# A cap of two gathers under way in the edge loops of a two-layer graph kernel

## The chip, the cores and the metric

The kernel runs on one core of one Trainium2 chip. The metric is the device time of one execution, in microseconds (us). Three runs of the kernel before gave a median of 5060.37 us (5058.44 to 5061.42).

## The reference

There are 6250 nodes with 128 features and 206,250 edges (100,000 random pairs in both directions, and one loop per node), sorted by destination. Two layers follow one another:

```
h = relu(layernorm(x))
# layer 0, per edge e = (row = src[e], col = dst[e]), 8 heads of 16
att = exp(clip(sum_d((h[row] @ Wq) * (h[col] @ Wk)), -10, 10))
res[row] += att / (sum of att over the row) * (h[col] @ Wv)
x = x + layernorm(res + h) * gamma + beta
h = relu(layernorm(x))
# layer 1
alpha = beta1 * dot(h[row], h[col]) / (|h[row]| |h[col]|)
out[row] = sum(softmax over the row's edges of alpha * h[col])
x = x + out
```

So each layer reads, for each edge, a whole row of a table by the edge's `col`.

## The kernel before

`sort_and_project` sorts the edges by `row` into tiles of 128 edges and makes the table `kv` (256 float32 per node) in DRAM. `layer0_edges` walks over the edges, `between_layers` makes the next table `h1` (130 float32 per node), `layer1_edges` walks over the edges again, and `finish` writes the output.

Both edge loops go over 417 groups (`GROUPS`) of `GT` = 4 tiles. For a tile, POOL issues one indirect DMA, a gather, that fetches 128 rows of the table into the 128 partitions of one slot of the ring `G` (`gather_groups`, line 892). The ring holds 8 groups in the first loop (`RING0`, tile name kv_rows) and 12 in the second (`RING1`, h_rows). The other engines work some groups behind, each by its own counted semaphores. `walk` writes one turn of the loop out in Python and repeats it with a hardware loop: the turn is 16 groups in the first loop (`HAND0`) and 24 in the second (`HAND1`), for POOL, DVE, ACT and SP.

Once a turn the last tile of the last group isn't gathered by POOL: SP fetches its 128 rows one by one into the buffer `hand` (`hand_rows`, lines 1023 and 1467; 8 of them per group in the first loop, up to 6 in the second), and ACT copies them into the ring (lines 1088 and 1522). `by_hand(u, t, period)` says whether a group is such a one. It then has three gathers, j = 0, 1, 2.

The order on POOL within a group is: wait until ACT has written the group's indices (`s_idx`), wait until the ring's slot is free (`s_read`: DVE's line 1195 in the first loop, PE's line 1586 in the second), add 1 to `s_go`, and then four gathers in a row with no wait between them. An addition to `s_go` is an instruction of its own on the queue, and the waits before it are on it. Each gather adds 16 to the semaphore of its ring slot (`s_gat[k]`, 8 semaphores in the first loop, 12 in the second), one for each of 16 DMA engines, when its data has landed. `gathers_of` counts how many gathers of the slot lie at or before a group, and DVE waits for 16 times that before the first use of the group (lines 1177 and 1657): in the first loop the product at line 1182, in the second the cosines at line 1633.

Of the kernel before, what the change touches and what calls it, by code (L numbers as in the profile page):

```python
# [45 lines left out]
GT = 4  # L46
# [9 lines left out]
HALF = UPG // 2  # L56
# [5 lines left out]
RING0 = 8  # L62
RING1 = 12
# [11 lines left out]
HAND0 = 16  # L75
BYHAND = P // HAND0
COPY0_AT = 12
HAND1 = 2 * RING1
# [791 lines left out]
    return u == period - 1 and not (isinstance(t, int) and t == 0)  # L870


def gathers_of(t, u, ring, period):

    each, now = GT * (period // ring), GT * (u // ring + 1)
    if u % ring < ring - 1 or isinstance(t, int) and t == 0:
        return each * t + now
    return (each - 1) * t + now + (u < period - 1)


def gather_groups(pool, ring, table, G, idx, s_idx, s_read, s_gat, s_go, period=None):

    def step(i, u, t):
        if not inside(i):
            return
        k = u % ring
        hand = period is not None and by_hand(u, t, period)
        pool.wait_ge(s_idx, i + 1)
        need(pool, s_read, i - ring + 1)
        pool.sem_inc(s_go, 1)  # L890
        for j in range(GT - hand):
            pool.indirect_dma_start(out=G[:, k, j, :], out_offset=None, in_=table,  # L892
                                    in_offset=bass.IndirectOffsetOnAxis(ap=idx[:, k, j:j + 1], axis=0)
                                    ).then_inc(s_gat[k], 16)
    walk(pool, step, period or ring, first=0, drain=0)


def own_quad(dram, q, n):
# [18 lines left out]
def layer0_edges(nc, mem, dram):  # L917

    with ExitStack() as ctx:
# [37 lines left out]
        s_across = sem("s_across")  # L957
        s_decoded = sem("s_decoded")
        s_idx = sem("s_idx0")
        s_gat = [sem(f"s_gat0_{k}") for k in range(RING0)]  # L960
        s_part = sem("s_part0")
        s_turned = sem("s_turned0")
        s_bytile = sem("s_bytile0")
# [174 lines left out]
        def _(dve):  # L1138
# [28 lines left out]
            def step(i, u, t):  # L1167
                if inside(i + 4):
                    k = u % NEAR
                    dve.wait_ge(s_spread, i + 5)  # L1170
                    need(dve, s_q, i + 5 - NEAR)
                    if inside(i):
                        dve.wait_ge(s_own, i + 1)
                    nc.vector.tensor_scalar(hotT[:, k, :], B_ps[u % 2], part_no[:, 0:1], None,
                                            ALU.is_equal).then_inc(s_hotT, 1)
                if inside(i):
                    dve.wait_ge(s_gat[u % RING0], 16 * gathers_of(t, u, RING0, HAND0))
                    if by_hand(u, t, HAND0):
                        dve.wait_ge(s_copied, t)
                    dve.wait_ge(s_q, i + 1)  # L1180
                    need(dve, s_red, i)
                    nc.vector.tensor_tensor(prod[:, :].rearrange("p (j f) -> p j f", f=D),
                                            Q_ps[u % NEAR].rearrange("p (j f) -> p j f", f=D),
                                            G[:, u % RING0, :, 0:D], ALU.mult).then_inc(s_prod, 1)
                if inside(i):
                    dve.wait_ge(s_prod, i + 1)
                    need(dve, s_clip, i + 1 - NEAR)
                    nc.vector.reduce_sum(att[:, u % NEAR, :],
                                         prod[:, :].rearrange("p (a d) -> p a d", d=HD), AX_X).then_inc(s_red, 1)
                if inside(i - 2):  # L1190
                    k = (u - 2) % NEAR
                    dve.wait_ge(s_ex, i - 1)
                    need(dve, s_sum, i - 1 - NEAR)
                    v = vx[:, k, :, :]
                    nc.vector.tensor_tensor(v[:, :, 0:D].rearrange("p j (h d) -> p j h d", d=HD),
                                            G[:, (u - 2) % RING0, :, D:2 * D].rearrange("p j (h d) -> p j h d", d=HD),
                                            v[:, :, D:AW0].unsqueeze(3).broadcast_to((P, GT, HEADS, HD)),
                                            ALU.mult).then_inc(s_vx, 1)
                if inside(i - 4):
                    for h in range(HALF):  # L1200
                        add_unit(i, u, t, h)
                if inside(i - 2):
                    nc.vector.tensor_tensor(hot[:, k, :].rearrange("p (j n) -> p j n", n=P),
                                            over(loc_f[:, ds(GT * (i - 2), GT)], P), under(iota[:, :], GT),
                                            ALU.is_equal).then_inc(s_hot, 1)
                if inside(i):
                    dve.wait_ge(s_red, i + 1)
                    need(dve, s_ex, i + 1 - NEAR)
                    nc.vector.tensor_scalar(clip[:, u % NEAR, :], att[:, u % NEAR, :], -10.0, 10.0,  # L1209
                                            ALU.max, ALU.min).then_inc(s_clip, 1)  # L1210
                if inside(i - 4):
                    for h in range(HALF, UPG):
                        add_unit(i, u, t, h)
# [159 lines left out]
def layer1_edges(nc, mem, dram):  # L1373
# [3 lines left out]
    with ExitStack() as ctx:  # L1377
# [44 lines left out]
        s_ids = sem("s_ids1")  # L1422
        s_hand = [sem(f"s_hand1_{k}") for k in range(2)]
        s_copied = sem("s_copied1")
        s_gat = [sem(f"s_gat1_{k}") for k in range(RING1)]
        s_own = [sem(f"s_own_{k}") for k in range(RING1 // FOUR)]
        s_hotT = sem("s_hotT1")
        s_hot = sem("s_hot1")
# [171 lines left out]
        def _(dve):  # L1600
# [38 lines left out]
            def step(i, u, t):  # L1639
                if inside(i - 9):  # L1640
                    for h in range(HALF):
                        add_unit(i, u, t, h)
                if inside(i - 6):
                    k = (u - 6) % SOON
                    dve.wait_ge(s_E, i - 5)
                    need(dve, s_wgt, i - 5 - SOON)
                    nc.vector.tensor_tensor(below[:, k, :], logit[:, (u - 6) % RING1, :], E_ps,
                                            ALU.subtract).then_inc(s_below, 1)
                if inside(i - 9):
                    for h in range(HALF, UPG):  # L1650
                        add_unit(i, u, t, h)
                if inside(i - 4):
                    dve.wait_ge(s_L, i - 3)
                    nc.vector.reduce_max(highs[:, ds(UPG * (i - 4), UPG), 1:2].rearrange("p u o -> p (u o)"),  # L1654
                                         L_ps[u % 2].rearrange("p (h e) -> p h e", h=UPG), AX_X).then_inc(s_gmax, 1)
                if inside(i):
                    dve.wait_ge(s_gat[u % RING1], 16 * gathers_of(t, u, RING1, HAND1))
                    if by_hand(u, t, HAND1):
                        dve.wait_ge(s_copied, t)
                    dve.wait_ge(s_q, i + 1)  # L1660
                    need(dve, s_logit, i + 1 - SOON)
                    need(dve, s_prod, i)
                    cosines(u, 0, GT // 2)
                if inside(i - 4):
                    w, v = (u - 4) % RING1, (u - 4) % SOON
                    before = 0.0 if isinstance(i, int) and i == 4 else tops[:, (u - 5) % RING1, UPG - 1, 1:2]
                    dve.wait_ge(s_gmax, i - 3)
                    need(dve, s_newtop, i - 4)
                    units = slice(UPG * (i - 4), UPG * (i - 3)) if isinstance(i, int) else ds(UPG * (i - 4), UPG)
                    nc.vector.tensor_tensor_scan(tops[:, w, :, :].rearrange("p u k -> p (u k)"),  # L1670
                                                 same[:, units, :].rearrange("p u k -> p (u k)"),
                                                 highs[:, units, :].rearrange("p u k -> p (u k)"),
                                                 before, ALU.mult, ALU.max).then_inc(s_newtop, 1)
                if inside(i):
                    cosines(u, GT // 2, GT).then_inc(s_prod, 1)
                if inside(i - 4):
                    dve.wait_ge(s_newtop, i - 3)
                    need(dve, s_corr, i - 3 - SOON)
                    nc.vector.tensor_tensor(fall[:, v, :], tops[:, w, :, 0:1].rearrange("p u o -> p (u o)"),
                                            tops[:, w, :, 1:2].rearrange("p u o -> p (u o)"),  # L1680
                                            ALU.subtract).then_inc(s_fall, 1)
                if inside(i):
                    need(dve, s_hotw, i + 1 - RING1)
                    nc.vector.tensor_tensor(hot[:, u % RING1, :, :], under(loc_b[:, ds(GT * i, GT)], P),
                                            iota_j[:, :, :], ALU.is_equal).then_inc(s_hot, 1)
# [93 lines left out]
```

## Time and profile before

| | |
|---|---|
| median of 3 runs | 5060.37 us |
| profiled execution: span on the page (it gives no other time) | 7130.1 us |
| first loop, first to last gather | 686.9 to 3894.4 us, 1643 gathers |
| second loop, first to last gather | 4052.2 to 7053.7 us, 1652 gathers |
| POOL, share of the span | 47% |
| PE, DVE, ACT | 61%, 58%, 34% |

The profiled execution is one run under the hardware profiler, and its span is 2070 us longer than the median. Its rows give durations and distances of single instructions. A row of the timeline is: start us, duration us, engine, line, operation, output<-input, and in brackets the idle time of the engine before it with what ended it.

### The profile page before, as it was taken

The numbers are of one execution on the slowest core, as the hardware profiler recorded it, in microseconds if no ns is written. First come the engines' busy times: TensorE is split into PE (matmuls) and PEld (weight loads), VectorE is DVE, ScalarE is ACT, GpSimd is POOL, SyncE is SP. The second block draws the span as 40 slices with busy tenths as digits, with TensorE's granted clock in tenths as the row PEclk, the third lists the DMA queues.
The fourth block names the chain that finished last, engine by engine and source line by source line (L and its number), as shares of the span: only waits on it lengthen the run. The fifth ranks groups of instructions, "written<-read, shape, count | busy, mean of one in ns | idle before, by whom it ended". The sixth has DMA issues, their size and how long they took to land. (4 is left out here: it accounts for less than half of the span.)

```text
span 7130.1 us, 118004 instructions
## 1 busy us (share of the span) xinstructions
PE 4342.2 (61%) x22945; PEld 3749.1 (53%) x22946; DVE 4103.2 (58%) x12176; ACT 2444.7 (34%) x8557; POOL 3380.1 (47%) x3426
## 2 busy tenths in 40 slices
PE   6997555555555555555455156677667676666665
PEld 3886344434443444434344156676666676666665
DVE  8998555555555555555556545555555555555555
ACT  4997111111110111111011544454454444444443
POOL 1334555545454554545454245555555555555552
PEclk8998666666666666666666576666676666776666
DMA  1001222222222222222222112121221121112111
GB/s 35 25 23 34 81 80 76 77 75 77 74 79 77 77 77 75 77 75 79 77 76 73 38 43 48 46 48 47 48 47 47 47 49 46 47 47 49 46 45 39
DMA packets 211652, 414.52 MB, mean 58 GB/s; under 512 B 69399, under 2 KB 103640, under 8 KB 211068
## 3 DMA queue, kind: packets, MB, share of 16 engines
q0 software_dynamic: 135184, 326.41, 17.4%
q1 hardware_dynamic: 74048, 79.04, 3.8%
q10 hardware_dynamic: 1836, 4.03, 0.2%
q14 instruction: 553, 4.53, 0.2%
q8 instruction: 31, 0.51, 0.0%
HBM read 363.52 MB, written 42.48 MB: 57 GB/s over the span
## 5 line engine op out<-in xcount | busy, mean ns | idle before, releaser
L892 POOL DMA_INDIRECT kv_rows<-kv_table,idx_ring x1643 | 1624.6, 989 | 1590.9 <-issue 1003.7
L892 POOL DMA_INDIRECT h_rows<-h_table,idx_ring x1652 | 1566.7, 948 | 1592.7 <-issue 1029.9
L1132 PE MATMUL psum<-vx,hot 128*128 128x136 f32 x3336 | 864.0, 411 | 1135.6 <-DVE acc L1165 1041.0
L1132 PEld LDWEIGHTS psum<-vx,hot 128*128 128x128 f32 x3336 | 696.2, 287 | 1280.3 <-DVE acc L1165 1140.8
L1628 DVE SCALAR_TENSOR_TENSOR h_sb<-h_sb,corr,psum 128x129 f32 x1668 | 582.8, 349 | 931.8 <-PE psum L1586 496.4
L1165 DVE TENSOR_TENSOR acc<-acc,psum 128x136 f32 x1668 | 489.4, 293 | 1006.2 <-remote 850.0
L1576 PE MATMUL psum<-ident,hotl 128*128 128x128 f32 x1668 | 393.9, 381 | 952.7 <-DVE highs L1654 880.6
L1080 ACT ACTIVATE vx<-clip 128x32 f32<-128x32 f32 x417 | 95.2, 229 | 2332.1 <-DVE clip L1209 1878.7
L1576 PEld LDWEIGHTS psum<-ident,hotl 128*128 128x128 f32 x1668 | 258.5, 192 | 1030.6 <-issue 895.4
L1121 PE MATMUL psum<-q_sb,hotT 128*128 x3336 | 712.0, 380 | 32.9 <-issue 23.0
L1121 PEld LDWEIGHTS psum<-q_sb,hotT 128*128 128x128 f32 x3336 | 607.5, 273 | 184.7 <-issue 184.7
L1586 PE MATMUL psum<-h_rows,hotw 128*128 128x129 f32 x3336 | 685.2, 373 | 3.3 <-DVE h_sb L1628 2.7
L1567 PE MATMUL psum<-q_sb,acc 128*128 x3336 | 634.8, 350 | 40.4 <-issue 21.5
L1515 ACT ACTIVATE logit<-cosb,cb_sb 128x4 f32<-128x4 f32 x417 | 124.0, 297 | 1559.6 <-DVE prod L1633 1313.2
L1586 PEld LDWEIGHTS psum<-h_rows,hotw 128*128 128x128 f32 x3336 | 650.1, 288 | 4.9 <-issue 3.3
L1594 PEld LDWEIGHTS psum<-tops,acc 128*128 128x128 f32 x3336 | 585.1, 263 | 0.0
L1567 PEld LDWEIGHTS psum<-q_sb,acc 128*128 128x128 f32 x3336 | 555.6, 251 | 42.9 <-issue 42.8
L1594 PE MATMUL psum<-tops,acc 128*128 128x1 f32 x3336 | 548.8, 286 | 0.0
L1507 ACT ACTIVATE hotl<-hot,logit 128x128 f32<-128x128 bf16 x1668 | 536.9, 392 | 0.0
L1507 ACT ACTIVATE hotw<-hot,wgt 128x128 f32<-128x128 bf16 x1668 | 536.2, 392 | 0.2
L1633 DVE SCALAR_TENSOR_TENSOR prod<-psum,h_rows 128x128 f32<-128x128 f32 x1668 | 509.5, 343 | 40.4 <-remote 35.5
L597 ACT ACTIVATE ends<-is_place,pk_now 128x96 f32<-128x96 bf16 x1260 | 460.7, 467 | 59.6 <-DVE is_place L771 58.0
(225 smaller groups left out, 5834.1 us busy)
## 6 DMA issues: line engine op xcount, KB each, us to landing
hand<-kv_table SPq DMA_DIRECT2D x3200, 1.0 KB
hand<-h_table SPq DMA_DIRECT2D x2048, 0.5 KB
own_rows<-own SPq DMA_DIRECT2D x104, 256.0 KB
own<-own_rows SPq DMA_DIRECT2D x104, 256.0 KB
h_rows<-h_table,idx_ring POOLq DMA_INDIRECT x1652
kv_rows<-kv_table,idx_ring POOLq DMA_INDIRECT x1643
kv_table<-kv SPq DMA_DIRECT2D x21, 256.0 KB, 2.1
out<-q_sb SPq DMA_DIRECT2D x2, 1536.0 KB
```

Of the source, the lines that this page charges most:

```text
L597: last = nc.scalar.activation(to_place[:, k, c, :], is_place[:, k, :, c], ACT.Copy, scale=pk_now[:, r, BATCH * b + c:BATCH * b + c + 1])
L892: pool.indirect_dma_start(out=G[:, k, j, :], out_offset=None, in_=table, in_offset=bass.IndirectOffsetOnAxis(ap=idx[:, k, j:j + 1], axis=0 ...
L1121: last = nc.tensor.matmul(Q_ps[k][:, j * P:(j + 1) * P], hotT[:, k, j * P:(j + 1) * P], q_sb[:, ds(blks[j], 1), :].rearrange("p o f -> p ( ...
L1132: last = nc.tensor.matmul(S_ps[j // HALF][:, j % HALF, :], hot[:, k, j * P:(j + 1) * P], vx[:, k, j, :], start=True, stop=True)
L1165: nc.vector.tensor_tensor(sums, sums, S_ps[h // HALF][:, h % HALF, :], ALU.add).then_inc(s_acc, 1)
L1507: last = nc.scalar.activation(out[:, j * P:(j + 1) * P], hot[:, u, :, j], ACT.Copy, scale=scale[:, j:j + 1])
L1567: last = nc.tensor.matmul(Q_ps[k][:, j * P:(j + 1) * P], hotT[:, (u + 1) % RING1, j * P:(j + 1) * P], q_sb[:, ds(blks[j], 1), :].rearrange ...
L1576: last = nc.tensor.transpose(L_ps[u % 2][:, j * P:(j + 1) * P], hotl[:, (u - 2) % TRIO, j * P:(j + 1) * P], ident[:, :])
L1586: last = nc.tensor.matmul(S_ps[j // HALF][:, j % HALF, :], hotw[:, (u - 8) % TRIO, j * P:(j + 1) * P], G[:, (u - 8) % RING1, j, 0:AW1], st ...
L1594: last = nc.tensor.matmul(E_ps[:, j:j + 1], hotT[:, n, j * P:(j + 1) * P], tops[:, n, j, 1:2], start=True, stop=True)
L1628: nc.vector.scalar_tensor_tensor(sums, sums, corr[:, (u - 9) % RING1, h:h + 1], S_ps[h // HALF][:, h % HALF, :], ALU.mult, ALU.add).then_i ...
L1633: last = nc.vector.scalar_tensor_tensor(prod[:, j * P:(j + 1) * P], Q_ps[u % 2][:, j * P:(j + 1) * P], G[:, u % RING1, j, D + 1:TW], G[:, ...
```

## The change

POOL gets a wait ahead of each gather. Gathers are split by the parity of their tile j in the group, and there are two semaphores, `s_gat[0]` for the even tiles and `s_gat[1]` for the odd ones, in place of one for each slot of the ring. Before the gather of tile j POOL waits until all gathers of the same parity issued so far have landed, and adds 1 to `s_go`. Only the first two gathers of a loop have no such wait. DVE's wait for a group becomes two waits, one for each parity. A group that is fetched partly by hand lacks its gather j = 3, an odd one. Nothing is changed in what is computed, in the ring's sizes or in the other engines.

```diff
-def gathers_of(t, u, ring, period):
+def gathers_of(t, u, period, parity):
 
-    each, now = GT * (period // ring), GT * (u // ring + 1)
-    if u % ring < ring - 1 or isinstance(t, int) and t == 0:
+    each, now = HALF * period, HALF * (u + 1)
+    if parity == 0 or isinstance(t, int) and t == 0:
         return each * t + now
     return (each - 1) * t + now + (u < period - 1)
 
+def landed(eng, s_gat, t, u, period):
+
+    for parity in range(2):
+        eng.wait_ge(s_gat[parity], 16 * gathers_of(t, u, period, parity))
...
         pool.sem_inc(s_go, 1)
+        asked = [gathers_of(t, u, period, parity) - HALF + (hand and parity == 1) for parity in range(2)]
         for j in range(GT - hand):
+            if j >= 2 or not (isinstance(i, int) and i == 0):
+                pool.wait_ge(s_gat[j % 2], 16 * (asked[j % 2] + j // 2))
+                pool.sem_inc(s_go, 1)
             pool.indirect_dma_start(out=G[:, k, j, :], out_offset=None, in_=table,
                                     in_offset=bass.IndirectOffsetOnAxis(ap=idx[:, k, j:j + 1], axis=0)
-                                    ).then_inc(s_gat[k], 16)
+                                    ).then_inc(s_gat[j % 2], 16)
...
-                    dve.wait_ge(s_gat[u % RING0], 16 * gathers_of(t, u, RING0, HAND0))
+                    landed(dve, s_gat, t, u, HAND0)
...
-                    dve.wait_ge(s_gat[u % RING1], 16 * gathers_of(t, u, RING1, HAND1))
+                    landed(dve, s_gat, t, u, HAND1)
```

## Rows read from the trace of the kernel before

**Rows 1.** The page's part 1: busy time, share of the span, instructions.
```profile
PE 4342.2 (61%) x22945; PEld 3749.1 (53%) x22946; DVE 4103.2 (58%) x12176; ACT 2444.7 (34%) x8557; POOL 3380.1 (47%) x3426
```

**Rows 2.** Line 892: duration ns min/median/max, first and last start us.
```profile
L892 POOL DMA_INDIRECT h_rows<-h_table,idx_ring x1652: 938/944/1855, 4052.2 to 7053.7; - x184
L892 POOL DMA_INDIRECT kv_rows<-kv_table,idx_ring x1643: 940/946/1725, 686.9 to 3894.4; - x183
```

**Rows 3.** Waits of all engines: waited for, us in total, times, longest us.
```profile
POOL kv_rows L892 <- DVE vx L1195: 580.0, 149, 15.3
...
ACT kv_rows L1088 <- DMA hand<-kv_table: 517.9, 24, 25.4
...
POOL h_rows L892 <- PE psum L1586: 335.4, 110, 7.3
...
DVE prod L1182 <- ACT kv_rows L1088: 264.8, 25, 13.3
```

**Rows 4.** Timeline, first loop: DVE's pace when it catches up, and SP's.
```profile
2004.44 0.75 DVE L1174 TENSOR_SCALAR hotT<-psum,part_no 128x512 f32<-128x512 f32 x1
...
2004.93 25.02 SPq L1023 DMA_DIRECT2D hand<-kv_table  x28
...
2009.00 0.75 DVE L1174 TENSOR_SCALAR hotT<-psum,part_no 128x512 f32<-128x512 f32 x1
```

**Rows 5.** Timeline of POOL, first loop: gathers in a row, then a pause.
```profile
2039.94 0.95 POOL L892 DMA_INDIRECT kv_rows<-kv_table,idx_ring  x1 [0.30 <-issue]
2041.19 0.95 POOL L892 DMA_INDIRECT kv_rows<-kv_table,idx_ring  x1 [0.30 <-issue]
2042.44 0.95 POOL L892 DMA_INDIRECT kv_rows<-kv_table,idx_ring  x1 [0.30 <-issue]
2043.69 0.94 POOL L892 DMA_INDIRECT kv_rows<-kv_table,idx_ring  x1 [0.30 <-issue]
2044.94 0.95 POOL L892 DMA_INDIRECT kv_rows<-kv_table,idx_ring  x1 [0.30 <-issue]
```

**Rows 6.** Quarter microseconds after the gather at 2044.94; DMA share and GB/s stand last.
```profile
2045.94:2046.19 0.25, 0.00 (x0) 0.00 (x0) 0.00 (x0) 0.00 (x0) 0.00 (x0) 0.50 0.07 21
...
2046.44:2046.69 0.25, 0.00 (x0) 0.00 (x0) 0.00 (x0) 0.00 (x0) 0.00 (x0) 0.50 0.43 98
...
2046.94:2047.19 0.25, 0.00 (x0) 0.00 (x0) 0.00 (x0) 0.00 (x0) 0.00 (x0) 0.50 0.49 197
2047.19:2047.44 0.25, 0.00 (x0) 0.00 (x0) 0.00 (x0) 0.00 (x0) 0.00 (x0) 0.50 0.02 0
2047.44:2047.69 0.25, 0.00 (x0) 0.00 (x0) 0.00 (x0) 0.00 (x0) 0.00 (x0) 0.50 0.00 0
```

**Rows 7.** The same in the second loop, after a last gather at 5412.87.
```profile
5414.62:5414.87 0.25, 0.00 (x0) 0.00 (x0) 0.00 (x0) 0.00 (x0) 0.00 (x0) 0.50 0.51 117
5414.87:5415.12 0.25, 0.00 (x0) 0.00 (x0) 0.00 (x0) 0.00 (x0) 0.00 (x0) 0.50 0.02 0
5415.12:5415.37 0.25, 0.00 (x0) 0.00 (x0) 0.06 (x1) 0.00 (x0) 0.00 (x0) 0.50 0.00 0
```

**Rows 8.** Timeline: from a releaser's end to the gather that it releases.
```profile
2052.37 0.68 DVE L1195 TENSOR_TENSOR vx<-kv_rows,vx 128x512 f32<-128x512 f32 x1
...
2053.86 1.26 POOL L892 DMA_INDIRECT kv_rows<-kv_table,idx_ring  x1 [7.98 <-DVE vx L1195]
...
5453.84 1.85 PE L1586 MATMUL psum<-h_rows,hotw 128*128 128x129 f32 x8
...
5456.51 0.94 POOL L892 DMA_INDIRECT h_rows<-h_table,idx_ring  x1 [2.33 <-PE psum L1586]
```

**Rows 9.** Timeline of POOL, second loop: the next two heads of groups after 5456.51.
```profile
5463.18 0.94 POOL L892 DMA_INDIRECT h_rows<-h_table,idx_ring  x1 [1.86 <-PE psum L1586]
...
5469.77 0.94 POOL L892 DMA_INDIRECT h_rows<-h_table,idx_ring  x1 [1.90 <-remote]
```

**Rows 10.** The page's costliest groups: busy, mean ns, idle before with its releaser.
```profile
L892 POOL DMA_INDIRECT kv_rows<-kv_table,idx_ring x1643 | 1624.6, 989 | 1590.9 <-issue 1003.7
```

More of the change, by code:

```diff
@@ L870, in by_hand, with gather_groups @@
     return u == period - 1 and not (isinstance(t, int) and t == 0)
-def gathers_of(t, u, ring, period):
-    each, now = GT * (period // ring), GT * (u // ring + 1)
-    if u % ring < ring - 1 or isinstance(t, int) and t == 0:
+def gathers_of(t, u, period, parity):
+    each, now = HALF * period, HALF * (u + 1)
+    if parity == 0 or isinstance(t, int) and t == 0:
         return each * t + now
     return (each - 1) * t + now + (u < period - 1)
-def gather_groups(pool, ring, table, G, idx, s_idx, s_read, s_gat, s_go, period=None):
+def landed(eng, s_gat, t, u, period):
+    for parity in range(2):
+        eng.wait_ge(s_gat[parity], 16 * gathers_of(t, u, period, parity))
+def gather_groups(pool, ring, table, G, idx, s_idx, s_read, s_gat, s_go, period):
     def step(i, u, t):
@@ L886, in step @@
         k = u % ring
-        hand = period is not None and by_hand(u, t, period)
+        hand = by_hand(u, t, period)
         pool.wait_ge(s_idx, i + 1)
@@ L890, in step @@
         pool.sem_inc(s_go, 1)
+        asked = [gathers_of(t, u, period, parity) - HALF + (hand and parity == 1) for parity in range(2)]
         for j in range(GT - hand):
+            if j >= 2 or not (isinstance(i, int) and i == 0):
+                pool.wait_ge(s_gat[j % 2], 16 * (asked[j % 2] + j // 2))
+                pool.sem_inc(s_go, 1)
             pool.indirect_dma_start(out=G[:, k, j, :], out_offset=None, in_=table,
                                     in_offset=bass.IndirectOffsetOnAxis(ap=idx[:, k, j:j + 1], axis=0)
-                                    ).then_inc(s_gat[k], 16)
-    walk(pool, step, period or ring, first=0, drain=0)
+                                    ).then_inc(s_gat[j % 2], 16)
+    walk(pool, step, period, first=0, drain=0)
 def own_quad(dram, q, n):
@@ L959, in layer0_edges @@
         s_idx = sem("s_idx0")
-        s_gat = [sem(f"s_gat0_{k}") for k in range(RING0)]
+        s_gat = [sem(f"s_gat0_{n}") for n in range(2)]
         s_part = sem("s_part0")
@@ L1424, in layer1_edges @@
         s_copied = sem("s_copied1")
-        s_gat = [sem(f"s_gat1_{k}") for k in range(RING1)]
+        s_gat = [sem(f"s_gat1_{n}") for n in range(2)]
         s_own = [sem(f"s_own_{k}") for k in range(RING1 // FOUR)]
```

## The prediction

> **What bounds the kernel now.** I read the page's busy shares first, then the gathers' line, the waits, and the timeline of POOL. No engine is full: POOL is busy 47% of the span, PE 61% [rows 1]. This page alone doesn't name the bound, since the profiled execution is 2070 us longer than the median of the runs. So the question is which part of the profile also holds without the profiler. In the timeline gathers that follow one another start 1.25 us apart: 0.95 us of work and 0.30 us between them [rows 5]. If the loops went at that pace throughout, they would take (1643 + 1652) x 1.25 = 4119 us [rows 2]. Outside them lie 686.9 us before the first gather, 157.8 us between the loops and 76.4 us from the last gather to the end of the span of 7130.1 us, 921 us together [rows 2]. The sum is 5040 us, 20 us under the measured median of 5060. I take it that in an ordinary run POOL's issue of gathers, 1.25 us each, is the bound in both loops from end to end.
>
> In the profiled execution it isn't: the first loop takes 3207.5 us for 417 groups, 7.7 us each, against 63 gathers of 1.25 us per 16 groups, 4.9 us each. POOL fills the ring and then waits for DVE and PE (580.0 and 335.4 us), ACT waits for the rows fetched by hand (517.9 us) and DVE for ACT (264.8 us) [rows 3]. SP's 28 small transfers take 25.02 us there, 0.89 us each and 7.1 us for the 8 of a group; DVE needs 4.56 us per group when it catches up [rows 4]. So rows of single instructions carry the sum, and the long idle times of this trace don't.
>
> **The change part by part.** The sum is the profiled execution's own rows at the pace without stalls, 5040 us, and the difference is put on the median, 5060. Its own time is the span, 7130.1 us; the page gives nothing around it.
>
> *The wait for the landing.* This is the whole effect. Gather n is released when gather n-2 has landed. What must pass between the starts of n-2 and n is the time from a gather's start to its landing, and the time from a release to the start of the released gather.
>
> Start to landing: after the last gather before a pause the DMA engines can be watched alone. For the gather at 2044.94 they carry its data from 2046.44 on and fall silent in the quarter that begins at 2047.19, 2.25 to 2.50 us after its start; the traffic up to 2046.19 belongs to the gather before [rows 6]. In the second loop, with rows of half the size, they fall silent 2.00 to 2.25 us after the start at 5412.87 [rows 7]. I take 2.40 and 2.20 us. These gathers had no successor behind them, so nothing in this time is a queue that a shallower queue would shorten.
>
> Release to start: the gather at 2053.86 starts 0.81 us after DVE's line 1195 ended (2052.37 + 0.68), the one at 5456.51 starts 0.82 us after PE's line 1586 ended (5453.84 + 1.85) [rows 8]. In the kernel before this time is hidden, since POOL's queue is worked ahead of the gathers; behind a wait that ends last it is exposed each time. That is 3.21 and 3.02 us. How long the semaphore takes to rise after the last traffic, no row shows. Its lower bound is 0; as its upper one I take 0.15 us, since the nearest row, DVE's end to POOL's start, is 0.81 us with the dispatch in it and leaves little room for a longer notice. I add 0.09 and 0.08 us and get 3.30 and 3.10 us for two gathers, 1.65 and 1.55 us for one, against 2.50 and 1.25 us. The wait therefore does end last, by 0.8 and 0.6 us.
>
> The count: even tiles are never taken out by hand, so each loop has a chain of 2 x 417 = 834 even gathers, each released by the one before. The odd chain has fewer and runs beside it. The loops take 834 x 3.30 = 2752 us and 834 x 3.10 = 2585 us, 5338 us together, against 4119. The change costs 1219 us, and the time is 5060 + 1219 = 6279 us.
>
> The Trainium skill (DMA: Bandwidth & Descriptors, section "Anatomy of one DMA — SWDGE (gpsimd) path") gives a DMA from this engine about 2.0 us fixed plus its bytes by 436e3 per us, and says that a wait on a semaphore stands on the issuing sequencer before dispatch. That is 2.30 us for 131,072 bytes and 2.15 us for 66,560, a little under the rows, and as an estimate the sum would come to 834 x (3.11 + 2.97) = 5071 us in the loops, some 6012 us in all. The rule speaks against the change as the rows do.
>
> *The added instructions on POOL.* One addition to `s_go` and one wait per gather, and the arithmetic of the waited value. Behind them on POOL's queue stand all later gathers, and for these DVE waits. At the head of a group POOL's queue already works through two waits and one addition, and gathers in a row keep their 1.25 us across the heads: of five in a row at least one is a head, and all five start 1.25 us apart [rows 5]. So they cost nothing beside a gather in progress. Behind a wait, only the addition that holds it lies on the path, and it is in the 0.81 us. Bounds: 0, and if all of it were exposed 0.1 us per step of the chain, 1668 x 0.1 = 167 us. I take 0.
>
> *DVE's wait becomes two.* 834 more waits. DVE needs 4.56 us per group [rows 4] and would get one every 6.6 and 6.2 us, so this is covered; without that cover it would be under 0.1 us per group, 80 us.
>
> *Fewer semaphores, by-hand groups.* The counting is exact for each parity, so a group is released with its own gathers and no other. After a by-hand group the next even gather waits for the gather just before it; it is in the even chain all the same and adds nothing.
>
> *What is late next.* In the second loop PE and its partners also set a pace: the heads of groups at 5456.51, 5463.18 and 5469.77 us lie 6.67 and 6.59 us apart in this profiled trace [rows 8, 9], more than the 6.2 us that the gathers would give. In ordinary runs this pace must be lower, since the median leaves only about 5 us per group. Slower arrival of work could bring some of it back. I leave it to the range and a rival.
>
> **The rivals.**
>
> 1. *The landing is hidden (about 5060 us).* If outside the profiler a gather landed 0.8 us sooner in the first loop and 0.6 us sooner in the second, the wait would be over before POOL gets to it. For it: the profiler does lengthen SP's transfers and perhaps every DMA. Against it: the gathers' own pace fits the unprofiled median to 20 us, and 1.5 us of the 2.4 pass before the first byte moves [rows 6], on POOL's side of the transfer. 4%.
>
> 2. *Faster (about 4990 us).* POOL's instructions average 989 ns in the first loop against a median of 946 (1624.6 us over 1643 gathers) [rows 2, 10]. If long ones came from several gathers under way at once, a cap would save up to 0.043 x 1643 = 71 us. It decides only where the two-gather chain is under 2.50 us. The landing rows stand against it. 2%.
>
> 3. *PE takes over in the second loop (about 6450 us).* If the slower arrival brings the second loop to the profiled pace of some 6.6 us, it takes 417 x 6.6 = 2752 us in place of 2585, 167 us more: 6446 us. The heads of [rows 9] speak for it. Against it: those groups follow stalls of the profiled execution, and an ordinary run does a group in 5 us. 15%.
>
> 4. *A short chain (about 5850 us).* The gathers land 0.25 us sooner without the profiler: 1668 x 0.25 = 417 us less, 5862 us. 14%.
>
> 5. *The cap isn't one of two.* If the counts let three through, three gathers would share 3.3 us, 1.1 us each, under 1.25, and nothing would change: 5060 us. The values in the diff are those of all earlier gathers of a parity, and the by-hand one is taken off. 1%.
>
> **How the numbers follow.** My forecast, 6279 us, has 64%. Its own ends: silence at 2.25 and 2.00 us after the start gives 834 x (3.06 + 2.82) = 4904 us and 5845 in all; silence at 2.50 and 2.25 us and 0.15 us to notice it gives 834 x (3.46 + 3.22) = 5571 us and 6512. With the short chain and PE's pace in it, the range is 5850 to 6520 us. A change of 0.2% (10 us) is about what a measurement of this kernel can tell from none. Slower: 64 + 15 + 14 = 93%. Same: rivals 1 and 5, 5%. Faster: 2%.
>
> **What would show it right or wrong.** In the new trace POOL's gathers should start about 1.65 us apart in the first loop and 1.55 us in the second, with 0.6 to 0.7 us of idle time before them instead of 0.30 us, ended by a gather's landing or marked as issue; their own 0.95 us should stay. Runs of gathers 1.25 us apart should be gone but for pairs: in an uneven chain one distance may be 1.25 us and the next 2.05. POOL's long waits for DVE and PE should shrink, since 6.6 us per group is close to the 7.7 us that the profiled first loop takes anyway. For the same reason the profiled span should grow far less than the median, to 7130 to 7700 us. If gathers still start 1.25 us apart, the landing is hidden and I am wrong. If they are 1.65 us apart but the median stays near 5060, POOL's issue was never the bound of ordinary runs.

## The result, and the profile after

The changed kernel takes 6800.83 us (median of 3 runs, 6793.10 to 6804.32), against 5060.37 us before. The ratio is 1.343, with a 95% interval of 1.342 to 1.345. The prediction was 6279 us, with a range of 5850 to 6520 us: the sign and the mechanism came as forecast, the size didn't. The change costs 1740 us where 1219 were expected.

The page of the new trace, its parts 1 and 5, with POOL's lines (busy, mean ns, idle before with its releaser), answers to [rows 1, 10]:

```profile
span 6802.6 us, 125599 instructions
...
PE 4908.2 (72%) x22945; PEld 4132.4 (61%) x22946; DVE 4139.0 (61%) x12176; ACT 2447.8 (36%) x8557; POOL 3328.7 (49%) x3426
...
L902 POOL DMA_INDIRECT kv_rows<-kv_table,idx_ring x1643 | 1580.5, 962 | 1482.2 <-DMA kv_rows<-kv_table,idx_ring 905.5
L902 POOL DMA_INDIRECT h_rows<-h_table,idx_ring x1652 | 1559.5, 944 | 1438.2 <-DMA h_rows<-h_table,idx_ring 850.5
```

Most of POOL's idle time is now ended by its own gathers (905.5 of 1482.2 us and 850.5 of 1438.2 us), as predicted. The view of waits also puts 234.9 us, 204 times, on ACT's write of the indices; that write isn't what POOL waits for, since ACT writes the indices of a group eight groups ahead, and from the ninth group on each is done at least 32 us before the group's first gather. The new line of the gathers (duration ns min/median/max, first and last start us), which answers to [rows 2], and what DVE waits for:

```profile
L902 POOL DMA_INDIRECT h_rows<-h_table,idx_ring x1652: 938/942/1857, 3872.0 to 6739.4; - x184
L902 POOL DMA_INDIRECT kv_rows<-kv_table,idx_ring x1643: 940/944/1662, 687.1 to 3741.8; - x183
...
  DVE prod L1192: 986.2, 411
  DVE prod L1643: 967.8, 408
```

The last two rows stand under "who waited for it": DVE now waits for the gathers in almost every group (411 and 408 times in 417). The loops take 3741.8 - 687.1 = 3054.7 us and 6739.4 - 3872.0 = 2867.4 us. Over the 834 even gathers of each that is 3.66 and 3.44 us per step of the chain, against 3.30 and 3.10 us in the prediction.

The timeline of POOL in the first loop answers to [rows 5]:

```profile
2000.32 0.95 POOL L902 DMA_INDIRECT kv_rows<-kv_table,idx_ring  x1 [0.30 <-issue]
2002.58 1.02 POOL L902 DMA_INDIRECT kv_rows<-kv_table,idx_ring  x1 [1.31 <-DMA kv_rows<-kv_table,idx_ring]
2003.91 0.94 POOL L902 DMA_INDIRECT kv_rows<-kv_table,idx_ring  x1 [0.30 <-issue]
2006.23 0.94 POOL L902 DMA_INDIRECT kv_rows<-kv_table,idx_ring  x1 [1.37 <-DMA kv_rows<-kv_table,idx_ring]
2007.47 0.95 POOL L902 DMA_INDIRECT kv_rows<-kv_table,idx_ring  x1 [0.30 <-issue]
```

The reader is to see two interleaved chains: each gather starts 3.56 to 3.65 us after the one two before it (2002.58 to 2006.23, 2003.91 to 2007.47). The gathers' own work stays at 0.95 us. Here the chains run unevenly, so that one distance is short, 1.24 to 1.33 us, and the next 2.3 us.

### The profile page after: what moved, and what is told of

It is laid out like the page before. It is cut to its first block and busy times, and to the rows that moved or that the text cites. A ratio compares the mean times of both kernels' runs of the same rounds, so it can differ in the third digit from the quotient of the medians.

```text
span 6802.6 us, 125599 instructions
## 1 busy us (share of the span) xinstructions
PE 4908.2 (72%) x22945; PEld 4132.4 (61%) x22946; DVE 4139.0 (61%) x12176; ACT 2447.8 (36%) x8557; POOL 3328.7 (49%) x3426
## 5 line engine op out<-in xcount | busy, mean ns | idle before, releaser
L902 POOL DMA_INDIRECT kv_rows<-kv_table,idx_ring x1643 | 1580.5, 962 | 1482.2 <-DMA kv_rows<-kv_table,idx_ring 905.5
L902 POOL DMA_INDIRECT h_rows<-h_table,idx_ring x1652 | 1559.5, 944 | 1438.2 <-DMA h_rows<-h_table,idx_ring 850.5
L1142 PE MATMUL psum<-vx,hot 128*128 128x136 f32 x3336 | 1051.4, 470 | 906.5 <-DVE acc L1175 883.5
L1142 PEld LDWEIGHTS psum<-vx,hot 128*128 128x128 f32 x3336 | 787.3, 321 | 1160.0 <-DVE acc L1175 1110.9
L1192 DVE TENSOR_TENSOR prod<-psum,kv_rows 128x512 f32<-128x512 f32 x417 | 288.5, 692 | 991.7 <-DMA kv_rows<-kv_table,idx_ring 986.2
L1131 PE MATMUL psum<-q_sb,hotT 128*128 x3336 | 861.0, 439 | 39.4 <-issue 38.9
L1131 PEld LDWEIGHTS psum<-q_sb,hotT 128*128 128x128 f32 x3336 | 739.2, 326 | 223.9 <-issue 223.9
L1577 PE MATMUL psum<-q_sb,acc 128*128 x3336 | 681.7, 368 | 204.7 <-DVE prod L1643 195.3
L1596 PE MATMUL psum<-h_rows,hotw 128*128 128x129 f32 x3336 | 724.6, 389 | 2.7 <-DVE h_sb L1638 2.7
L1577 PEld LDWEIGHTS psum<-q_sb,acc 128*128 128x128 f32 x3336 | 590.1, 265 | 223.0 <-issue 221.6
L1596 PEld LDWEIGHTS psum<-h_rows,hotw 128*128 128x128 f32 x3336 | 693.5, 305 | 4.4 <-issue 3.3
```

The costliest lines, as they stand in the source:

```text
L1131: last = nc.tensor.matmul(Q_ps[k][:, j * P:(j + 1) * P], hotT[:, k, j * P:(j + 1) * P], q_sb[:, ds(blks[j], 1), :].rearrange("p o f -> p ( ...
L1142: last = nc.tensor.matmul(S_ps[j // HALF][:, j % HALF, :], hot[:, k, j * P:(j + 1) * P], vx[:, k, j, :], start=True, stop=True)
L1577: last = nc.tensor.matmul(Q_ps[k][:, j * P:(j + 1) * P], hotT[:, (u + 1) % RING1, j * P:(j + 1) * P], q_sb[:, ds(blks[j], 1), :].rearrange ...
L1596: last = nc.tensor.matmul(S_ps[j // HALF][:, j % HALF, :], hotw[:, (u - 8) % TRIO, j * P:(j + 1) * P], G[:, (u - 8) % RING1, j, 0:AW1], st ...
```

## The experiments

**The kernel before, again.** The first trace had a span 2070 us over the median, and the whole baseline was an inference from it. No edit.

> The kernel before, unchanged, for a second trace. Theory (POOL's issue bounds ordinary runs, and the stalls of the first trace belong to that one execution): span near 5060 us, gathers 1.25 to 1.27 us apart in both loops, POOL never waiting for DVE or PE for long. Rival (the stalls belong to every profiled execution of this kernel): span near 7130 us again, with pauses of 7 to 8 us, and then the trace says nothing of what bounds the timed runs.

Measured: 5063.70 us, span 5061.9 us. Line 892 of this second trace, then waits of all engines:

```profile
L892 POOL DMA_INDIRECT h_rows<-h_table,idx_ring x1652: 940/944/1854, 2928.2 to 4998.6; - x184
L892 POOL DMA_INDIRECT kv_rows<-kv_table,idx_ring x1643: 942/946/1722, 687.5 to 2798.3; - x183
```

```profile
POOL h_rows L892 <- issue: 485.6, 1593, 0.3
POOL kv_rows L892 <- issue: 469.9, 1541, 0.3
```

POOL issues without a pause: 1541 and 1593 gathers have 0.3 us of idle time at most before them, and what else it waits for within the loops is no longer than that. The loops take 2110.8 and 2070.4 us, 1.285 and 1.254 us per gather, the first a little over the 1.25 to 1.27 us expected; outside them lie 880.7 us. So POOL's issue does bound the kernel before, as the prediction inferred, and the pauses of 7 to 8 us belonged to that one execution; what caused them stays open. The changed kernel adds 943.9 us in the first loop and 797.0 us in the second.

**One gather under way.**

```diff
-            if j >= 2 or not (isinstance(i, int) and i == 0):
-                pool.wait_ge(s_gat[j % 2], 16 * (asked[j % 2] + j // 2))
+            if j >= 1 or not (isinstance(i, int) and i == 0):
+                for q in range(2):
+                    pool.wait_ge(s_gat[q], 16 * (asked[q] + (j + 1 - q) // 2))
```

> Each gather waits for all before it. Theory (two gathers share one full path of landing, notice and release, 3.66 us in the first loop and 3.44 us in the second on average, and don't slow one another): each gather takes that whole path, 1643 x 3.66 + 1652 x 3.44 = 11,696 us in the loops and 880 us outside, 12,580 us; as an alone gather meets less disturbance, 12,300 to 12,600 us. Rival (with two under way each lands later because of the other, and the forecast of 3.30 and 3.10 us was right for one alone): 5422 + 5121 + 880 = 11,420 us.

Measured: 12,412.59 us (one run), inside the 12,300 to 12,600 us of the theory. Line 903 gives both loops; below it stand two gathers of each loop in the timeline, and the step from one to the next:

```profile
L903 POOL DMA_INDIRECT h_rows<-h_table,idx_ring x1652: 942/942/1200, 6744.8 to 12347.6; - x184
L903 POOL DMA_INDIRECT kv_rows<-kv_table,idx_ring x1643: 944/944/1671, 687.0 to 6614.4; - x183
```

```profile
2000.59 0.95 POOL L903 DMA_INDIRECT kv_rows<-kv_table,idx_ring  x1 [2.57 <-DMA kv_rows<-kv_table,idx_ring]
2004.19 0.95 POOL L903 DMA_INDIRECT kv_rows<-kv_table,idx_ring  x1 [2.65 <-DMA kv_rows<-kv_table,idx_ring]
...
8002.69 0.94 POOL L903 DMA_INDIRECT h_rows<-h_table,idx_ring  x1 [2.49 <-DMA h_rows<-h_table,idx_ring]
8006.02 0.94 POOL L903 DMA_INDIRECT h_rows<-h_table,idx_ring  x1 [2.38 <-DMA h_rows<-h_table,idx_ring]
```

A gather alone takes 5927.4 / 1642 = 3.61 us and 5602.8 / 1651 = 3.39 us on average. This is all but 0.05 us of the step of two under way (3.66 and 3.44 us), and the rival, 3.30 and 3.10 us for a gather alone, falls. Two gathers hardly slow one another.

This trace also shows the term by itself, because nothing else moves. In stretches of 0.05 us, DMA share and GB/s last, after the gather at 2000.59 and after the one at 8002.69:

```profile
2002.85:2002.90 0.05, 0.00 (x0) 0.00 (x0) 0.00 (x0) 0.00 (x0) 0.00 (x0) 0.50 0.24 82
2002.90:2002.95 0.05, 0.00 (x0) 0.00 (x0) 0.00 (x0) 0.00 (x0) 0.00 (x0) 0.50 0.01 0
2002.95:2003.00 0.05, 0.00 (x0) 0.00 (x0) 0.00 (x0) 0.00 (x0) 0.00 (x0) 0.50 0.02 0
2003.00:2003.05 0.05, 0.00 (x0) 0.00 (x0) 0.00 (x0) 0.00 (x0) 0.00 (x0) 0.50 0.01 0
2003.05:2003.10 0.05, 0.00 (x0) 0.00 (x0) 0.00 (x0) 0.00 (x0) 0.00 (x0) 0.50 0.00 0
```

```profile
8004.80:8004.85 0.05, 0.00 (x0) 0.00 (x0) 0.00 (x0) 0.00 (x0) 0.00 (x0) 0.50 0.03 0
8004.85:8004.90 0.05, 0.00 (x0) 0.00 (x0) 0.00 (x0) 0.00 (x0) 0.00 (x0) 0.50 0.01 0
8004.90:8004.95 0.05, 0.00 (x0) 0.00 (x0) 0.00 (x0) 0.00 (x0) 0.00 (x0) 0.50 0.01 0
8004.95:8005.00 0.05, 0.00 (x0) 0.00 (x0) 0.00 (x0) 0.00 (x0) 0.00 (x0) 0.50 0.00 0
```

A packet counts in the stretch in which it starts. The last one with data starts before 2002.90; small packets with a share but next to no bytes follow, the last of them before 2003.05, 2.41 to 2.46 us after the gather's start. In the second loop the last falls before 8004.95, 2.21 to 2.26 us after the start. These are the 2.40 and 2.20 us of the prediction. The next gather starts 1.14 to 1.19 us later in the first loop and 1.07 to 1.12 us later in the second. With 0.81 and 0.82 us from release to start [rows 8], 0.33 to 0.38 and 0.25 to 0.30 us are left between the last traffic and the release. The prediction had 0.09 and 0.08.

The same trace also records each update of a semaphore and each DMA packet, which no view lists. There the path splits without a difference. Medians over the gathers of each loop, in us:

| | first loop | second loop | prediction |
|---|---|---|---|
| start to the end of the gather's last packet | 2.40 | 2.20 | 2.40, 2.20 |
| last packet to the sixteenth update of the semaphore | 0.34 | 0.33 | 0.09, 0.08 |
| last update to the next gather's start | 0.82 | 0.82 | 0.81, 0.82 |
| step from gather to gather | 3.56 | 3.34 | 3.30, 3.10 |

Of the three parts only the second is more than 0.01 us from the prediction. The means of the whole step, 3.61 and 3.39 us, lie above its medians.

DVE, which waits for the same landing, sees it late too:

```profile
2003.42 0.69 DVE L1193 TENSOR_TENSOR prod<-psum,kv_rows 128x512 f32<-128x512 f32 x1 [9.55 <-DMA kv_rows<-kv_table,idx_ring]
```

It starts 0.37 to 0.42 us after the last packet, on an engine with no dispatch of a DMA in its way.

**Three and four gathers under way.** The semaphores are one for each tile of a group (four); gather n waits for n-3 or n-4.

```diff
-            if j >= 2 or not (isinstance(i, int) and i == 0):
-                pool.wait_ge(s_gat[j % 2], 16 * (asked[j % 2] + j // 2))
+            if not (isinstance(i, int) and i == 0 and j < BEHIND):
+                q = (j - BEHIND) % GT
+                pool.wait_ge(s_gat[q], 16 * (asked[q] + (j >= BEHIND)))
```

> Gather n waits for gather n-3, with one semaphore for each tile of a group. Theory (only the path over the cap counts): 3.66 and 3.44 us shared by three are 1.22 and 1.15 us, just under the 1.25 us of POOL's issue; with late landings now and then 5080 to 5250 us. Rival (the added wait, addition and arithmetic cost some 0.15 us for each gather, which would be the part of the slowdown that the forecast lacked): at least 3295 x 0.15 = 494 us more, 5550 us or more.

> Gather n waits for gather n-4; the same instructions as with three. Theory: 3.66 and 3.44 us shared by four are 0.92 and 0.86 us, far under 1.25 us, so that the waits are over before POOL comes to them and the time is that of the kernel before, 5050 to 5075 us. Rival (the added instructions cost 0.15 us for each gather): 5550 us.

Measured: three, 5247.20 us (5235.83 to 5255.55), ratio 1.036 (1.034 to 1.038), at the upper end of what the theory gave, 187 us over the kernel before. Four, 5103.45 us (5101.35 to 5105.51), ratio 1.009 (1.007 to 1.010), 28 us over the theory's range and far under the rival. So the cap decides, not the instructions that were added with it; but four still cost 43 us. POOL's timeline under the cap of four, with the gathers counted between pauses in the second fence (the count in brackets after the fifth number is POOL's):

```profile
830.78 0.94 POOL L904 DMA_INDIRECT kv_rows<-kv_table,idx_ring  x1 [0.30 <-issue]
833.24 0.94 POOL L904 DMA_INDIRECT kv_rows<-kv_table,idx_ring  x1 [1.51 <-issue]
...
974.68 0.95 POOL L904 DMA_INDIRECT kv_rows<-kv_table,idx_ring  x1 [0.30 <-issue]
976.81 0.94 POOL L904 DMA_INDIRECT kv_rows<-kv_table,idx_ring  x1 [1.18 <-issue]
...
1401.75 0.95 POOL L904 DMA_INDIRECT kv_rows<-kv_table,idx_ring  x1 [0.30 <-issue]
1404.24 0.94 POOL L904 DMA_INDIRECT kv_rows<-kv_table,idx_ring  x1 [1.55 <-issue]
```

```profile
833.20:976.80 143.60, 109.43 (x476) 83.98 (x476) 120.28 (x280) 24.15 (x86) 108.86 (x110) 0.71 0.40 116
976.80:1404.20 427.40, 324.41 (x1423) 248.22 (x1422) 361.70 (x838) 71.46 (x255) 322.32 (x329) 0.73 0.40 117
```

110 gathers lie between the first two pauses and 329, about 3 x 110, between the second and the third listed. So once in 110 gathers POOL stands for 0.9 to 1.25 us more than usual. The trace has 14 such pauses in each loop, the first after 113 gathers, 28 in all. They lengthen the loops by some 31 us together, out of the 43 us. The same pause is longer with two under way:

```profile
892.33 0.94 POOL L902 DMA_INDIRECT kv_rows<-kv_table,idx_ring  x1 [0.37 <-issue]
897.23 0.94 POOL L902 DMA_INDIRECT kv_rows<-kv_table,idx_ring  x1 [3.96 <-issue]
...
1105.81 0.94 POOL L902 DMA_INDIRECT kv_rows<-kv_table,idx_ring  x1 [3.71 <-issue]
```

The sequencer's records in the same traces, which no view lists, say what it is: from the end of a wait to the sequencer's next instruction behind the gather 0.54 us pass as a rule, and 3.26 us (3.2 with four under way) once in 112 gathers with one and two under way and once in 110 with three and four, 14 times a loop. Such a long dispatch makes the loop 2.7 us longer with one or two under way and about 2.1 us with three, where the 28 of them make some 60 of the 187 us. The rest of the 187 us wasn't taken apart.

**The additions alone, and a cap that lets the queue run ahead.** Two tests of that reading: the first adds only the instructions, the second the full set of waits, but for the group two before.

```diff
# the kernel before, with the additions alone
         for j in range(GT - hand):
+            pool.sem_inc(s_go, 1)
# the kernel before, with waits for the group two before
         for j in range(GT - hand):
+            if not (isinstance(i, int) and i < 2):
+                back = (t, u - 2) if u >= 2 else (t - 1, u - 2 + period)
+                pool.wait_ge(s_gat[(k - 2) % ring], 16 * gathers_of(*back, ring, period))
+                pool.sem_inc(s_go, 1)
```

> The kernel before, with one more addition to the counter ahead of each gather and no wait on a landing. Four under way cost 43 us more than the kernel before. Theory (those 43 us are about 30 long dispatches, one after each 110 gathers and some 3.3 us in place of 0.55 us, which a queue worked far ahead hides and a cap of four doesn't quite): without the waits POOL's queue runs ahead again, 5055 to 5070 us. Rival (the added instructions cost 43 us, 0.013 us for each gather): 5100 us.

> The kernel before, with a wait and an addition ahead of each gather as in the change, but the wait is for the whole group two before (5 to 8 gathers under way). Theory of the long dispatches: POOL's queue may run at least 5 gathers ahead, more than 3.3 us, so that they are hidden again, 5055 to 5070 us. Rival (a wait, an addition and their arithmetic cost 43 us): 5100 us.

Measured: 5061.60 us, ratio 1.0000 (0.9991 to 1.0010), and 5062.61 us, ratio 1.0004 (0.9994 to 1.0013). A wait, an addition and their arithmetic for each of 3295 gathers cost nothing that can be measured where the queue is ahead, and with 5 to 8 gathers under way the long dispatches are hidden too: no two gathers of a loop start more than 2.2 us apart there.

**No rows by hand, under the cap of two.** `by_hand` returns False and SP fetches no rows.

> The changed kernel, with all tiles gathered by POOL and none fetched by hand: 25 more gathers in the first loop and 16 in the second, all odd, and no small transfers by SP. Theory (the chain of the 834 even gathers of each loop sets the time): 6780 to 6815 us, no more than with them; a little less if SP's small transfers disturbed the landings. Rival (the time goes by the number of gathers): 25 x 1.83 + 16 x 1.72 = 73 us more, 6874 us.

Measured: 6831.00 us (6828.04 to 6833.98), 30 us over the changed kernel and outside both expectations. Its line of the gathers, against 3054.7 and 2867.4 us:

```profile
L900 POOL DMA_INDIRECT kv_rows<-kv_table,idx_ring x1668: 940/944/1717, 686.0 to 3740.1; - x186
L900 POOL DMA_INDIRECT h_rows<-h_table,idx_ring x1668: 938/942/1856, 3870.3 to 6769.1; - x186
```

The first loop takes 3054.1 us, the same with 25 more gathers; the second 2898.8 us, 31 us more. That left open whether 16 more gathers or something else cost 31 us, so both kernels were run again beside one another.

> The changed kernel, unchanged, beside the one without rows by hand on the same chip. Without them it had taken 30 us more, all of it in the second loop, where gathers landed some 0.03 us later; the cap in the second loop alone had the same 30 us too many. Theory (the even chain sets the time, and the 30 us are a difference between chips or placements in how soon a gather lands): both kernels come out within 15 us of one another, whatever their level between 6800 and 6840 us. Rival (the 16 more gathers cost 30 us in the second loop): 6800 us here, 30 us under the other.

> All tiles gathered by POOL under the cap of two, again. Theory: within 15 us of the changed kernel beside it. Rival: 30 us above it.

Measured: the changed kernel 6833.05 us (6830.93 to 6835.10), the one without rows by hand 6839.23 us (6831.33 to 6840.87), ratios 1.349 and 1.350 to the kernel before on that chip, with overlapping intervals. The theory holds: 41 more gathers change nothing beyond 6 us; all of them are odd. The level of the changed kernel itself moves by 32 us, from 6800.83 to 6833.05 us, while the kernel before moves from 5060.37 to 5064.14 us beside it. The traces show where: in the second loop of the first trace a gather's semaphore has its sixteenth update 2.50 us after the start (median), in the second loops of the four later traces with this cap in that loop 2.54 us. Over 834 steps 0.03 to 0.04 us are some 30 us. In the first loop all have 2.75 to 2.76 us. Why gathers landed later there stays open.

**The cap in one loop only.** The other loop keeps the functions of the kernel before.

```diff
# cap in the first loop only
-            gather_groups(pool, RING1, dram["h1"], G, idx, s_idx, s_sum, s_gat, s_go, HAND1)
+            gather_groups_free(pool, RING1, dram["h1"], G, idx, s_idx, s_sum, s_gat, s_go, HAND1)
-                    landed(dve, s_gat, t, u, HAND1)
+                    dve.wait_ge(s_gat[u % RING1], 16 * gathers_of_slot(t, u, RING1, HAND1))
```

> The cap of two in the first loop only. Theory (each loop pays its own chain, and no other engine is a bound): the first loop takes 3055 us in place of 2111 us, so 5061 + 944 = 6005 us; the second loop's POOL rows are those of the kernel before. Rival (PE at a lower granted clock carries part of the second loop's slowdown, or the loops' losses aren't additive): the two losses, of this run and of the rest of 1740 us, don't come out as 944 and 797 us; this one would be above 6030 or below 5980 us.

> The cap of two in the second loop only. The cap in the first loop alone cost 950 us of 1740. Theory (each loop pays its own chain): 2867 us in place of 2070 us for the second loop, 5061 + 797 = 5858 us, and the two losses sum to the whole within 20 us. Rival (PE's granted clock, low after a slow first loop, carries part of the second loop's loss in the changed kernel): under 5830 us here.

Measured: first loop only, 6011.37 us, ratio 1.188 (1.185 to 1.190); second loop only, 5887.33 us, ratio 1.162 (1.158 to 1.165). The uncapped second loop behind a capped first one, and the capped second loop behind an uncapped first one:

```profile
L927 POOL DMA_INDIRECT h_rows<-h_table,idx_ring x1652: 940/944/1854, 3874.2 to 5945.1; - x184
```

```profile
L902 POOL DMA_INDIRECT h_rows<-h_table,idx_ring x1652: 941/946/1856, 2928.4 to 5823.9; - x184
```

The first takes 2070.9 us, as in the kernel before (2070.4). The second takes 2895.5 us. That is 28 us over the expectation and close to the second loops of the other later traces (2890.9 to 2903.7 us). The losses are 950 us and, against the 5070.63 us beside it, 817 us (826 against the usual 5061): 1767 to 1776 us together, against 1769 us for the changed kernel when it was run again (6833.05 - 5064.14). Against the 1740 us of its first runs they are 27 to 36 us too many, outside the 20 us that was expected; that is the later landing of the second loop. With it they add up, and an uncapped second loop behind a slow first one loses nothing, so no other engine carries a part.

## Why the prediction was wrong in size

*The baseline: right.* POOL's issue bounds ordinary runs in both loops. The rows gave 921 us outside the loops, and by putting the difference on the median the forecast kept 941 (5060 less 4119); the second trace has 880.7. The gathers take 1.285 us in the first loop rather than 1.25. The two nearly cancel before the change; after it only the first counts, 61 us too much in the forecast.

*Start to the last traffic: right.* 2.40 and 2.20 us were taken, and the medians of a gather alone are 2.40 and 2.20 us.

*Release to start: right.* 0.81 and 0.82 us were taken from releases by DVE and PE; behind a landing it is 0.82 us in both loops.

*The notice of a landing: this term was mis-sized.* The prediction said "I add 0.09 and 0.08 us" and took 0.15 us as the upper bound, because 0.81 us from DVE's end to POOL's start "leaves little room for a longer notice". That row is of a release by an engine; it says nothing of how late a DMA's landing shows at a semaphore. The gather alone measures 0.34 us in the first loop and 0.33 in the second (medians; the means are 0.35 and 0.34). The notice therefore lacked 0.26 us in each step of either loop, 834 x 0.52 = some 430 us. By the whole step the forecast of 3.30 and 3.10 us lacks 0.31 and 0.29 us against a gather alone (3.61 and 3.39 us on average), 259 + 242 = 501 us, and against two under way 0.36 and 0.34 us, 584 us.

*The long dispatches: a term left out.* 28 of them at 2.72 us are 76 us, by the sequencer's records. Nothing of them stood in the prediction.

*Late landings: a small term left out.* 584 - 430 - 76 = 78 us remain. I took single rows of gathers with nothing behind them, and no allowance for landings that come late now and then. The median distance from a gather to the one two behind it, 3.56 and 3.32 us, is within 0.03 us of the median step of a gather alone, so these 78 us come from the few late ones; what makes them late wasn't taken apart.

The sum: 6279 + 430 + 76 + 78 - 61 = 6802 us, against 6802.6 us of span. It has to come out, since the 78 us are what was left over; the 430 and the 76 us are measured by themselves.

*The count of 834: right*, by the pair of runs without rows by hand. *The instructions cost nothing: right* (5061.60 and 5062.61 us), though no row stood behind the 0.1 us per step of its upper bound. *DVE's second wait is covered: right*, since DVE waits for gathers in nearly every group.

*The rivals.* The hidden landing and the faster kernel fell with the timeline. What spoke for the hidden landing was that the profiler lengthens SP's transfers; the second profiled trace doesn't bear that out, since 32 of them take 15.9 us there, 0.50 us each, where the first had 28 in 25.02 us. The short chain fell too: a gather's traffic ends as late as forecast, not 0.25 us sooner. PE's pace in the second loop fell too: the loops' losses add up, and a second loop behind a slowed first one keeps 2070.9 us. The cap is one of two: caps of one, two and three gave 12,412.59, 6800.83 and 5247.20 us. What the Trainium skill gives in the section cited (2.30 and 2.15 us) is below the traces' start to last traffic, and further below the 2.74 and 2.53 us from a gather's start to the last update of its semaphore. The estimate of 6012 us by it lies further off than the forecast; the measurement decides.

*The profiled span: wrong.* 7130 to 7700 us was forecast, 6802.6 us came. I took the stalls of the first trace for a property of profiled executions. The second trace of the same kernel has none. The range was drawn as if notices were bounded by 0.15 us; the largest unknown of the sum had the narrowest bound.

## What to carry to other kernels

A cap of n transfers under way can cost nothing only if n times the issue interval exceeds the whole path from the start of one to the start of the one that waits for it: work on the issuing engine, the transfer, the notice and the dispatch, here 3.4 to 3.7 us against 1.25. Near that limit leave some room for disturbance: three under way were on average enough here, and still cost 3.6%; four cost 0.9%, and five to eight nothing. When a wait that was hidden becomes the one that ends last, bound each hop that no row shows by a row of its own kind, and where there is none leave the range open on that side. And where a profiled span and the median are far apart, ask for a second trace before reading anything from its idle times.

## What the runs showed of the hardware that wasn't expected

- With one gather under way, 0.34 and 0.33 us (medians of the two loops) pass from the end of a gather's last packet to the last of the sixteen updates of its semaphore. In the gather shown above DVE and POOL's wait both go on 0.02 us after it, and POOL's next gather starts 0.82 us after it.
- POOL's sequencer takes 3.26 us over a dispatch in place of 0.54 us once in 112 gathers (one and two under way) or once in 110 (three and four), for rows of 1024 and of 520 bytes alike, by the sequencer's records. Each costs 2.7 us with one or two under way, about 2.1 with three and 1.1 with four. With 5 to 8 under way nothing is lost. What it does in that time wasn't tested.
- The same capped kernel came out at 6800.83 and 6833.05 us in two sets of runs, while the kernel before moved from 5060.37 to 5064.14 us beside it (5070.63 us in the runs beside the cap in the second loop). In the capped second loop gathers landed 0.03 to 0.04 us later, and a chain of 834 steps adds that up.
